# Self-attention in spells of a whole chunk, and cross-attention values in rounded parts

## The reference

```
h = ln(x, g1, be1);  x = attn(h, h, Wq1, Wk1, Wv1, Wo1, bo1) + x         # 1024 keys
h = ln(x, g2, be2);  x = attn(h, context, Wq2, Wk2, Wv2, Wo2, bo2) + x   # 64 keys
h = ln(x, g3, be3);  a, gate = split(h @ Wp + bp)                        # 2 x 1024
x = a * gelu(gate) @ W2 + b2 + x
attn: softmax(q k^T / 8) v, heads side by side, then @ Wo + bo
```

## Time and profile before

| | |
|---|---|
| median of 3 runs | 2184.45 us |
| the profiled execution: time, span | 2183.68 us, 2181.9 us |
| TensorE (PE) busy, share | 2152.3 us, 99% |
| DVE, ACT, POOL busy, share | 1448.5 (66%), 1030.8 (47%), 1394.8 (64%) us |
| self-attention's value products, first to last | 78.8 to 1639.6 us |
| cross-attention, first score product to the last out2's end | 1640.8 to 1904.6 us |
| ACT exponential of a round, mean | 1026 ns x 512 |
| ACT and DVE parts of a projection's split, mean | 599 and 681 ns x 120 |
| POOL scaling of an output chunk, mean | 1302 ns x 64 |
| DVE inverse of a quarter of the sums, mean | 921 ns x 256 |
| DVE copy of four turned tiles, mean | 630 ns x 32 |
| granted clock of TensorE, mean | 0.998 |

### The profile page before, as it was taken

The page is one execution under the profiler, slowest core; times in us unless marked ns, Lnnn a source line. Parts: engine busy times, 40 slices in busy tenths (PEclk is TensorE's granted clock), DMA queues, the critical chain, the costliest instruction groups (busy, mean ns, idle before and its releaser), DMA issues.

```text
span 2181.9 us, 31941 instructions
## 1 busy us (share of the span) xinstructions
PE 2152.3 (99%) x12244; PEld 1420.4 (65%) x12244; DVE 1448.5 (66%) x2491; ACT 1030.8 (47%) x1732; POOL 1394.8 (64%) x737
## 2 busy tenths in 40 slices
PE   7999999999999999999999999999999999999999
PEld 6555555566555556665555566555557888888888
DVE  5677777756776776567677756766776677654443
ACT  4444545533444554334446533444564556543332
POOL 2588788866788887668788866877885366200000
PEclk9999999999999999999999999999999999999999
DMA  6300000000100000010000000101000411001100
GB/s 213 116 6 15 6 6 20 6 6 1 58 6 5 6 15 6 6 44 15 11 6 16 5 6 1 49 6 25 1 20 20 134 55 45 1 3 38 39 11 30
DMA packets 46072, 58.75 MB, mean 27 GB/s; under 512 B 5856, under 2 KB 40288, under 8 KB 44768
## 3 DMA queue, kind: packets, MB, share of 16 engines
q1 hardware_dynamic: 45920, 56.71, 8.3%
HBM read 38.88 MB, written 17.83 MB: 26 GB/s over the span
## 4 chain that ended last, share of the span: by engine, by line
PE 97%; DVE 2%; ACT 1%; DMA 0%; issue 0%; POOL 0%; SPq 0%
PE attn_out L514 21%; PE score L498 18%; PE score L608 8%; PE first_score L469 8%; PE project L442 7%; PE score L502 6%; PE score L568 4%; PE first_score L535 4%; PE first_score L454 4%; PE project L594 3%; PE attn_out L594 3%; PE first_score L525 3%; PE attn_out L622 2%; PE project L622 2%; PE first_score L582 1%; PE first_score L482 1%
## 5 line engine op out<-in xcount | busy, mean ns | idle before, releaser
L797 DVE TENSOR_REDUCE nmax<-first_score 128x1 f32<-128x512 f32 x1024 | 681.8, 690 | 222.6 <-PE first_score L469 199.3
L1301 POOL TENSOR_TENSOR acc<-acc,pT_first 128x1024 f32<-128x1024 f32 x256 | 608.9, 2379 | 172.1 <-ACT pT_first L1117 142.5
L498 PE MATMUL score<-qk 64*128 64x512 f32 x3072 | 540.6, 400 | 0.5 <-ACT pT_more L1117 0.2
L498 PEld LDWEIGHTS score<-qk 64*128 64x128 f32 x3072 | 342.1, 184 | 109.3 <-ACT pT_first L1117 36.2
L1117 ACT ACTIVATE pT_first<-score 128x1024 f32<-128x1024 f32 x342 | 349.5, 1026 | 125.6 <-PE score L502 107.6
L469 PE MATMUL first_score<-qk 64*128 64x512 f32 x1024 | 377.2, 431 | 10.4 <-DVE hT L750 8.5
L1301 POOL TENSOR_TENSOR acc<-acc,pT_more 128x1024 f32<-128x1024 f32 x128 | 305.0, 2383 | 85.5 <-ACT pT_more L1117 70.8
L514 PE MATMUL attn_out<-pT_first,vT 128*64 128x512 f32 x1368 | 325.4, 601 | 0.0
L820 DVE RECIPROCAL inv<-sums 128x128 f32<-128x128 f32 x256 | 225.0, 921 | 123.3 <-ACT sums L1133 123.3
L502 PE MATMUL score<-shift,pick 64*128 64x512 f32 x1024 | 287.6, 392 | 0.0
L1095 ACT ACTIVATE qk<-project 128x512 fp32r<-128x512 f32 x120 | 71.9, 599 | 334.5 <-PE project L442 334.5
(11 more groups left out here) (175 smaller groups left out, 2780.0 us busy)
## 6 DMA issues: line engine op xcount, KB each, us to landing
xres<-x_middle SPq DMA_DIRECT2D x10, 512.0 KB, 3.8
xres<-in_x SPq DMA_DIRECT2D x4, 1024.0 KB, 6.7
raw_qk<-in_L_xattn_Wq SPq DMA_DIRECT2D x32, 128.0 KB, 2.3
raw_qk<-in_L_xattn_Wk SPq DMA_DIRECT2D x32, 128.0 KB, 2.5
raw_v<-in_L_xattn_Wv SPq DMA_DIRECT2D x8, 512.0 KB, 4.1
keys_all<-keys SPq DMA_DIRECT2D x1, 4096.0 KB, 11.3
values_all<-values SPq DMA_DIRECT2D x1, 4096.0 KB, 12.4
out_x<-xres SPq DMA_DIRECT2D x8, 512.0 KB, 2.9
```

Of the source, the lines that this page charges most:

```text
L498: e.matmul(bank, qk[P % 2][r, 2 + h, keys], qk[P % 2][r, w, queries], start=(part == 0), stop=False)
L797: e.tensor_reduce(nmax[:, t % 2, half, head:head + 1], FS[:, head * BANK:(head + 1) * BANK], AX.X, ALU.max, negate=True).then_inc(s.row_ma ...
L1301: e.tensor_tensor(total, total, p_tile(R), ALU.add).then_inc(s.probs_added, 1)
```

## The change

- A spell is a whole chunk: 40 steps, eight rounds. `PASSES` has eight first-pass steps per head.
- Head 0's first pass goes to T0 and T1, head 1's to PV and PJ, which are now one tensor of two banks. DVE reduces 1024 columns in one instruction into `maxima`; `gather_max` is gone. `shift` and `maxima` have one buffer.
- All eight rounds' value products follow the spell, into S0a, then the sums of the chunk before. The exponentials' ring has 8 buffers, the values' ring 8.
- One slot per chunk, with two projections (into PJ and S1b) and, ahead of them, what the two slots had, in PV, S0b and S1a. The first pair's two extra projections stand ahead of the first spell.
- The inverse is one instruction of 512 columns, two chunks behind. The last keys' split stands ahead of the inverse in the last spell.
- Cross-attention: the turned probabilities and the values are split into a rounded part and a rest (ACT copies, DVE or POOL subtracts), and `out2` is 24 matmuls of one pass each. ACT takes sums for heads 0 to 3 only, DVE for 4 to 15. Buffers are laid out anew, and some loads wait for other events.

```
-        PASSES = ((0, 6, 11, 17), (0, 9, 14, 19))
+        PASSES = ((4, 5, 12, 13, 23, 24, 34, 35), (4, 5, 18, 19, 29, 30, 38, 39))
+        PASS_BANKS = (("T0", "T1"), ("PV", "PJ"))
+        PASS_PAIRS = (FS, PX)
...
+        def slot(C):
+            P, c = divmod(C, CHUNKS)
+            (b, n), D = divmod(C, BC), C // (4 * CHUNKS)
+            jobs = [("max", C + 1, "T1")] if C + 1 < NC else []
+            between = []
+            if n - BC + 4 in range(CHUNKS):
+                between += [("ln", next_norm(b, n - BC + 4), k) for k in range(KT)]
+            if b and n in (1, 2):
+                between += [("out1", b - 1, TPC * (n - 1) + t) for t in range(TPC)]
+            if C % (4 * CHUNKS) == 4 * CHUNKS - 1 and D + 1 < GROUPS:
+                between += [("v", D + 1, jt) for jt in range(TILES)]
+            jobs += [(*job, ("PV", "S0b", "S1a")[i % 3]) for i, job in enumerate(between)]
+            after = P + 1 + c
+            if after < B * PAIRS:
+                jobs += [("qk", after, 1 - c, "PJ"), ("qk", after, 3 - c, "S1b")]
+            return jobs
...
             def first_score(C, t, half, head):     # TensorE
+                bank = PASS_BANKS[head][half]
...
+                last.then_inc(first_scored[head], 1)
+                free[bank] = ((s.row_max, passed(C, t, head)),)
...
+            for C in range(NC):                    # TensorE
+                parts, firsts = [0, 0], [0, 0]
+                for n in range(5 * TILES):
+                    for head in range(2):
+                        if n not in PASSES[head]:
+                            score(TILES * C + parts[head] // 4, parts[head] % 4, head)
+                            parts[head] += 1
+                        elif C + 1 < NC:
+                            first_score(C + 1, firsts[head] // 2, firsts[head] % 2, head)
+                            firsts[head] += 1
+                if C == NC - 1:
+                    sum_keys(C - 1, "T0")
+                for jt in range(TILES):
+                    attend(TILES * C + jt)
+                if 0 < C < NC - 1:
+                    sum_keys(C - 1, "T0")
+                whole_array(slot(C))
...
+            def row_max(C, t, head):               # DVE
+                need.wait_ge(first_scored[head], 2 * TPC * C + 2 * t + 2)
+                need.wait_ge(s.max_turned, C)
+                need.wait_ge(s.const, 8)
+                e.tensor_reduce(maxima[:, head * DH + t:head * DH + t + 1], PASS_PAIRS[head][:, :], AX.X, ALU.max,
                                 negate=True).then_inc(s.row_max, 1)
...
             def exponential(R):                    # ACT
+                if R >= TILES:
+                    need.wait_ge(s.attended, R - TILES + 1)
+                    need.wait_ge(s.probs_added, (TILES - 1) * (R // TILES - 1) + max(jt, 1))
+                e.activation(pT[:, jt].rearrange("p h n -> p (h n)"), SC[R % 2][:, :], ACT.Exp
...
             def out2(i):                           # TensorE
-                for p in range(PAIRS):
-                    last = e.matmul(banks[bank][:, 0:DIM], turned[i % 3][:, p, :], values[j % 2][:, p, :],
-                                    start=(p == 0), stop=(p == PAIRS - 1))
+                for n, (w, v) in enumerate(TERMS):
+                    if w:
+                        need.wait_ge(s.p2T_v, 2 * i + 2)
+                    if v:
+                        need.wait_ge(s.values2_lo, 2 * (j + 1))
+                    for p in range(PAIRS):
+                        last = e.matmul(banks[bank][:, 0:DIM], turned[i % 3][w][:, p, :], values[j % 2][v][:, p, :],
+                                        start=(n == p == 0), stop=(n == 2 and p == PAIRS - 1))
...
             def turn2(i):                          # DVE
-                e.tensor_copy(turned[i % 3][:, 4:8, :].rearrange("p j n -> p (j n)"), banks["T1"]
-                              ).then_inc(s.p2T_v, 1)
+                for half in range(2):
+                    hi, lo = (part[:, 4 * half:4 * half + 4, :].rearrange("p j n -> p (j n)") for part in turned[i % 3])
+                    need.wait_ge(s.p2T_a, 2 * i + half + 1)
+                    e.tensor_tensor(lo, banks[f"T{half}"], hi.bitcast(F32), ALU.subtract).then_inc(s.p2T_v, 1)
```

More of the change, by code:

```diff
@@ L285, in next_norm @@
             return (1, CHUNKS * (b + 1) + c) if b + 1 < B else (2, c)
[L287 to L326, removed]
@@ L501, in score @@
                     need.wait_ge(s.const, 8)
-                    e.matmul(bank, pick[r, :], shift[r, C % 2, :], start=False, stop=True).then_inc(s.scored, 1)
+                    e.matmul(bank, pick[r, :], shift[r, :], start=False, stop=True).then_inc(s.scored, 1)
                     free[f"S{R % 2}" + "ab"[head]] = ((s.exponential, R + 1),)
@@ L510, in attend @@
                 if jt == 0:
[L511 removed]
+                    bank_free("S0a")
                 for head in range(2):
                     c0 = p * PART + head * DH
[L514 to L515 removed]
+                    last = e.matmul(banks["S0a"][head * DH:(head + 1) * DH, :], vT[:, v_slot(D, jt), c0:c0 + DH],
+                                    pT[:, jt, head, :], start=(jt == 0), stop=(jt == TILES - 1))
                 last.then_inc(s.attended, 1)
                 if jt == TILES - 1:
[L518 removed]
+                    free["S0a"] = ((s.oT_written, C + 1),)
             def sum_keys(C, bank="PJ"):
@@ L970, in _ @@
                     out1(B - 1, i, ("PJ", "PV")[i % 2])
-                if i == 1:
-                    for quarter in range(4):
-                        invert_sums(NC - 1, quarter)
+                if i == 2:
+                    invert_sums(NC - 1)
                 if i in (TPC, 2 * TPC):
@@ L1147, in split_keys, with split_values @@
                 e.copy(hi, lo.bitcast(F32)).then_inc(s.keys2_hi, 1)
+            def split_values(j, half):
+                hi, lo = (part[:, 4 * half:4 * half + 4, :] for part in values[j % 2])
+                need.wait_ge(s.values2_loaded, 32 * (j + 1))
+                if j == 1:
+                    need.wait_ge(s.out1_product, NT)
+                e.copy(hi, lo.bitcast(F32)).then_inc(s.values2_hi, 1)
             def exponential2(i):
@@ L1156, in exponential2 @@
                 need.wait_ge(s.max_turned, NC)
-                if i == 2:
-                    need.wait_ge(s.oT_scaled, NC)
                 need.wait_ge(s.soft_inverse, max(i - 1, 0))
                 for h in range(HB):
-                    last = e.activation(P3[:, h], s3[:, h], ACT.Exp, bias=nm[:, h:h + 1], accum_out=ls[:, h:h + 1])
+                    last = e.activation(P3[:, h], s3[:, h], ACT.Exp, bias=nm[:, h:h + 1],
+                                        accum_out=ls[:, h:h + 1] if h < HA else None)
                 last.then_inc(s.exp2_first, 1)
@@ L1166, in turn2 @@
             def turn2(i):
-                need.wait_ge(s.turned2, 2 * i + 1)
                 need.wait_ge(s.out2_product, max(i - 2, 0))
-                e.copy(turned[i % 3][:, 0:4, :].rearrange("p j n -> p (j n)"), banks["T0"]).then_inc(s.p2T_a, 1)
+                for half in range(2):
+                    need.wait_ge(s.turned2, 2 * i + half + 1)
+                    e.copy(turned[i % 3][0][:, 4 * half:4 * half + 4, :].rearrange("p j n -> p (j n)"),
+                           banks[f"T{half}"]).then_inc(s.p2T_a, 1)
             def ffn_up(c, f):
@@ L1320, in split_keys, with split_values @@
                     last.then_inc(s.keys2_lo, 1)
+            def split_values(j, half):
+                hi, lo = (part[:, 4 * half:4 * half + 4, :] for part in values[j % 2])
+                need.wait_ge(s.values2_hi, 2 * j + half + 1)
+                e.tensor_tensor(lo, lo.bitcast(F32), hi.bitcast(F32), ALU.subtract).then_inc(s.values2_lo, 1)
             def split_ffn(n):
@@ L1372, in _ @@
                     scale2(i - 1)
+                if i < NT and i % TILES in (1, 2):
+                    split_values(i // TILES, i % TILES - 1)
                 if i == 2:
```

342 lines of the change are left out of this document (140 added, 202 removed).

## The result

The changed kernel takes 2212.35 us (2211.68 to 2213.71, 4 runs) where the kernel before took 2184.15 in the same series (2183.18 to 2185.07, 4 runs): a ratio of 1.013 [1.0112, 1.0148], slower by 28 us. The forecast was slower by 66. The profiled execution took 2212.11 us, its span is 2210.3, 28.4 more than before.

What follows compares the result with a forecast made beforehand. TensorE, 97% of the chain, was taken as the bound, with waits for ACT's exponential lengthening the spell. 2183.7 + 88 - 7 - 1.2 + 1 - 14.5 + 1 + 0 = 2251, forecast as 2250 us; range 2190 to 2282.

Steps and rivals of the forecast that it cites:

- The 1.53 us from a last step to the next round but one: Self-attention spell: least time from a round's last step start to the first step reusing its banks, 6.6 steps.
- TensorE takes its queue in order, so a wait of one head's matmul holds both heads: Self-attention spell: a late matmul delays both heads; waits 1.84 us plus six times 0.11, 2.5 a spell.
- the walk: Step-by-step timing of the 40-step self-attention spell: 12.1 us, making a chunk 23.2, 1.4 more than before, +88 in all.
- lockstep: Self-attention spell: both heads start each step together; for equally spaced first passes its own difference gave 2143 us.
- Rival A: Self-attention: the waits do not come, if the 1.53 us shrinks or a late head leaves the other running; 2094 us, 13%.
- 1.22 to 1.25 for a reduction of 1024 columns: DVE's wide first-pass reduction in self-attention, taken at 1.25 us, making head 0's step 12 0.1 late.
- -7 for the layer norm's turns and -1.2 for the keys: Turns leave T0 and T1, where the first pass waited: -7 us; cross-attention key splits move ahead of the inverse: -1.2.
- Start-up +1: Before the first spell: two projections only move ahead, and the last two reductions leave about +1 us.
- Cross-attention -14.5 and +1: Cheaper out2 saves 18.6 us, less 4 for DVE's norm rows: -14.5; copy and subtractions after the last tile: +1.
- the loop's +4: Cross-attention's loop through DVE and ACT: 0.2 us a tile over 24 tiles without out1, for DVE's norm rows.
- Feed-forward 0: Feed-forward stage: no step of the forecast gave it any change in time.
- rival B: Self-attention: slower but less, the exponential nearer 0.98 us and the tails of waits small; 2207 us, 20%.

Runs made afterwards that it cites:

- The reversed order: Changed kernel with head 1's matmul issued before head 0's in each of the 40 steps: 2249.44 us, ratio 1.0295 to the kernel before.
- the even places: Changed kernel with first passes at equal distances (head 0: 4, 5, 14, 15, 24, 25, 34, 35; head 1: 4, 5, 18, 19, 28, 29, 38, 39): 2159.55 us.

## Why the prediction came out too high

- **The 1.53 us from a last step to the next round but one: right.** 1064.08 to 1065.58 is 1.50; where the last step is itself the first after a wait it is 1.62 (1061.20 to 1062.82, 1065.58 to 1067.20). The longest wait stands where the forecast put it, ahead of head 1's round 6. The exponential's length as the price of the longer spell was right too; it is what the shortened exponentials took away.
- **"TensorE takes its queue in order, so a wait of one head's matmul holds both heads": this is the step that failed.** The queue does hold both heads, but the walk made of it that both start each step together, so that head 0's next step comes 0.34 after the late one of head 1. In the trace it starts with the late one, in two places of the spell. The walk ends round 2 at 4.08 us into the spell, measured 3.81; round 4 at 7.02, measured 6.69; round 5 at 8.89, measured 8.19. By that head 1's step 34 is 0.12 late and not 0.36. The waits came to 1.8, not 2.5: 0.70 of the chunk's 0.87 too much. The other 0.17 are the value products, 6.91 us (1046.46 to 1053.37) and not 4 x 1.77. Times 63, 0.87 is 55 us, 44 of them the spell's, where the whole error is 39. The reversed order (+37 us) shows the step; the even places, at the expected 2160 where lockstep had 2143, bear it out. Rival A had named the case as one of its two conditions ("a late head to leave the other running"), but as one that ends the waits; a head runs ahead by one step only and is then held. The Trainium skill states a part of this: "TensorEngine Tiling (Array Packing)", section Key Properties, has it that different tiles can load weights and multiply in parallel, independently. What a wait in the one queue does to the other tile the section does not say; the rows at 1065.58 show it.
- **1.22 to 1.25 for a reduction of 1024 columns: right.** DVE's rows at L759 have 1.22 and 1.23. The one wait that the forecast gave to it, 0.1 us ahead of step 12, is there too, at 1060.35 (14.5 us in 59 such waits in all):
```profile
1060.35 0.18 PEld L434 LDWEIGHTS first_score<-qk 64*128 64x128 f32 x1 [0.24 <-DVE maxima L759]
```
- **-7 for the layer norm's turns and -1.2 for the keys: wrong, about +1 together.** The waits for `hT` after the turns are 4.8 us in place of 8.5, eight in both kernels, but one is 3.1 us, and what follows it is slow:
```profile
383.11 0.96 PE L460 MATMUL score<-qk 64*128 64x512 f32 x5 [0.23 <-DVE hT L712]
...
1639.10 1.37 PE L460 MATMUL score<-qk 64*128 64x512 f32 x5 [3.07 <-DVE hT L712]
1639.85 1.05 PE L464 MATMUL score<-shift,pick 64*128 64x512 f32 x2
...
1640.00:1644.00 4.00, 4.00 (x26) 2.98 (x22) 2.38 (x3) 1.75 (x2) 0.00 (x0) 0.64 0.02 4
```
The granted clock is 0.64 over the next 4 us, a mixture of the 1.2 GHz level and 2.4 GHz, after 3 us in which TensorE stood; at 4 x 0.36 that is, as an estimate, some 1.4 us more. Each chunk with turns takes 1.51 us over one without (370.56 to 394.40 is 23.84), of which the turns themselves are 0.79; the wait at 383.11 is in the rest. No run takes the turns' cost by itself in either kernel, so how the missing 8 divide stays open beyond that.
- **Start-up +1: too small, +3.9.** Ahead of the first spell only one value projection lies between a pass and the one that needs its banks again, and the wide reduction is in the open. Three times a pass of head 1 waits for it, so that two value projections and the passes between them take 4.96 us (62.12 to 67.08) where they took 4.04, and once the maxima's turn does:
```profile
67.08 0.50 PE L434 MATMUL attn_project<-qk 64*128 64x512 f32 x1 [0.43 <-DVE maxima L759]
...
77.01 0.33 PE L444 MATMUL first_score<-ident,maxima 128*128 128x128 f32 x1 [0.85 <-DVE maxima L759]
```
- **Cross-attention -14.5 and +1: right, -14.1.** `out2` is the 2.87 forecast for 24 from the down product; the loop's +4 came as waits for POOL's scaling (3.0 us in three waits), not for DVE.
- **Feed-forward 0: wrong, +4.1,** with some 4 more inside the other stages: the place of the weights.

In one sum, forecast +67.3 against +28.4: the chunk -54.6, turns and keys +9.3, start-up +2.9, cross-attention -0.6, feed-forward +4.1. The forecast's range reaches from 2190 to 2282 and holds the time, but by luck: it was widened downward for rival B (a shorter exponential and small tails), which is not what happened. ACT's mean is 1026 ns, as before, and the first step after a wait still takes 0.34.

## What to carry to other kernels

When two halves of the array work side by side, walk each half with its own clock: a wait holds all that is queued behind it, but what the other half was given ahead of it goes, and its next matmul starts together with the late one. Which head comes first in a step is then a choice worth a run. And before a long spell is given up, try where its fillers stand: six places in a list were worth 53 us here, twice what the change had cost. When a stage whose code did not change gets slower by 1 to 2%, compare the means of its matmuls and put back the bytes that a removed buffer took.

## What the runs showed of the hardware

- The fp32r product of `hT` with weights, 128x128 by 512 columns, has a mean of 390 or 395 ns by the place of buffers in SBUF alone: 32 bytes give or take 8.6, 7.1 and 10.4 us in three kernels. For the feed-forward's up products 0, 64 and 96 bytes are the slow places with this layout, 32 the fast one; for the first scores of cross-attention 96 is fast as well (400 ns against 402).
- Rows 0 to 63 and 64 to 127 of TensorE run a whole step (0.23 us) apart under one instruction queue after a wait of the second head: its late matmul and the first head's next one both start at 1065.58. Which head issues first is worth 37 us in 2212.
- An exponential of 128x256 takes 0.38 us and one of 128x1024 1.03, yet shortening it moves the kernel with long spells by 95 us and the one with short spells by 17, with ACT busy for 47% in both.
